# A fused perceiver layer on one core: another order of the first groups, of the passage between the stages and of the first loads

## What is computed

```python
# 1 cross attention of the normalised x (hc) with the context (hq)
Sim = (hc @ w1)[:, :, None] + (hq @ w2)[:, None, :] + einsum('bid,bjd->bij', hc * w3, hq) + b_sim[0]
hq_hat = softmax(Sim, axis=2) @ hq
hc_bar = softmax(max(Sim, axis=2), axis=1) @ hc
x = x + concat([hc, hq_hat, hc * hq_hat, hc * hc_bar]) @ W_qv + b_qv
# 2 gated linear recurrence over the 32 tokens, then a layer norm
xg = ln(x) * sigmoid(ln(x) @ Wg.T + bg)
s = s @ A + xg[t] * Bp;  y[t] = s @ Cp + Dp * xg[t]
x = x + ln(y + xg) * gamma + beta
# 3 feed-forward with ternary weights and a low-rank term
h = bitlinear(ln(x), w_fc) + gate * (ln(x) @ v.T @ fast_b.T @ u.T)
x = x + bitlinear(relu(h) ** 2, w_proj)
```

## Time and profile before

| | before |
|---|---|
| median of three runs | 493.66 us (492.95 to 495.50) |
| profiled execution: time / span | 493.86 us / 492.0 us |
| mean granted clock of TensorE | 0.995 |
| PE busy | 463.0 us (94%) |
| PE weight loads busy | 400.3 us (81%) |
| DVE / ACT / POOL busy | 397.6 / 362.6 / 340.6 us |
| moved by DMA | 70.40 MB, mean 143 GB/s |

### The profile page before, as it was taken

The page is one execution under the profiler, slowest core; times in us unless marked ns, Lnnn a source line. Parts: engine busy times, 40 slices in busy tenths (PEclk is TensorE's granted clock), DMA queues, the critical chain, the costliest instruction groups (busy, mean ns, idle before and its releaser), DMA issues. The chain is left out here.

```text
span 492.0 us, 13707 instructions
## 1 busy us (share of the span) xinstructions
PE 463.0 (94%) x4375; PEld 400.3 (81%) x4375; DVE 397.6 (81%) x1210; ACT 362.6 (74%) x882; POOL 340.6 (69%) x446
## 2 busy tenths in 40 slices
PE   4889999999999999999999999778999999999995
PEld 3578788888988989888898878666888888888884
DVE  2698888888989889889889875788768788797654
ACT  3768688787887878878788786646787786876752
POOL 2478897876767767677676776124889887887552
PEclk9999999999999999999999998999999999999999
DMA  6954575576847648566674756774011312301102
GB/s 218 312 183 137 164 233 163 193 217 167 239 142 204 187 138 237 150 193 183 169 215 129 194 130 163 141 250 148 0 47 40 88 40 48 87 10 35 44 1 85
DMA packets 77454, 70.40 MB, mean 143 GB/s; under 512 B 39476, under 2 KB 60232, under 8 KB 76872
## 3 DMA queue, kind: packets, MB, share of 16 engines
q1 hardware_dynamic: 77384, 69.54, 49.2%
HBM read 56.87 MB, written 12.65 MB: 141 GB/s over the span
## 5 line engine op out<-in xcount | busy, mean ns | idle before, releaser
L1871 POOL TENSOR_TENSOR sq_lo<-scan_x,sq_hi 128x512 fp32r<-128x512 f32 x63 | 82.9, 1318 | 32.8 <-ACT sq_hi L1826 32.8
L1026 ACT COPY ctxT<-turn_ps 128x512 f32<-128x512 f32 x128 | 68.9, 590 | 10.2 <-PE turn_ps L801 3.8
L1818 ACT ACTIVATE relu<-fc_ps,fc_square 128x512 f32<-128x512 f32 x64 | 43.8, 686 | 32.7 <-PE fc_ps L1740 32.6
L1916 DVE SCALAR_TENSOR_TENSOR scan_x<-fc_ps,relu 128x512 f32<-128x512 f32 x64 | 43.7, 685 | 26.0 <-ACT relu L1818 25.4
L1209 POOL TENSOR_TENSOR hb_lo<-hbT,hb_hi 128x256 fp32r<-128x256 f32 x32 | 24.2, 758 | 43.0 <-ACT hb_hi L1097 43.0
L1734 PE MATMUL fc_ps<-xn_hi,fc_T 128*128 128x512 f32 x128 | 51.6, 403 | 2.1 <-DVE scan_x L1916 2.1
L1195 POOL TENSOR_TENSOR rstd<-ve,neg_half 128x1 f32<-128x1 f32 x64 | 35.3, 552 | 23.1 <-DVE ve L1456 20.7
L801 PE MATMUL turn_ps<-ident,ctxn 128*128 128x128 f32 x352 | 49.1, 285 | 2.3 <-DMA ctxn<-in_ctx 1.7
L1734 PE MATMUL fc_ps<-xn_lo,fc_T 128*128 128x512 f32 x128 | 50.4, 394 | 0.0
L1201 POOL TENSOR_TENSOR proj_in<-proj_in,below 128x512 f32<-128x512 f32 x31 | 48.6, 1567 | 0.0
L801 PEld LDWEIGHTS turn_ps<-ident,ctxn 128*128 128x128 f32 x352 | 42.7, 151 | 2.9 <-DMA ctxn<-in_ctx 2.1
(11 more groups left out here) (253 smaller groups left out, 1448.0 us busy)
## 6 DMA issues: line engine op xcount, KB each, us to landing
ctxn<-in_ctx SPq DMA_DIRECT2D x22, 1024.0 KB, 5.5
toeplitz<-in_ctx SPq DMA_DIRECT2D x10, 1024.0 KB, 5.6
resid<-in_x SPq DMA_DIRECT2D x32, 128.0 KB, 5.5
ctx_end<-in_ctx SPq DMA_DIRECT2D x32, 128.0 KB
gated_tokens<-gated SPq DMA_DIRECT2D x32, 128.0 KB, 6.0
scan_x<-gated_tokens SPq DMA_DIRECT2D x60, 64.0 KB, 4.8
out<-resid SPq DMA_DIRECT2D x7, 512.0 KB, 3.3
scan_quarters<-scan_x SPq DMA_DIRECT2D x3, 1024.0 KB, 5.4
```

What stands on the lines that cost most here:

```text
L1026: act.copy(ctxT[:, b, :, 0:J - 1], turn_ps[b % 2][:, :].rearrange("p (k j) -> p k j", k=KD)).then_inc(ctxT_copied, 1)
L1818: act.activation(relu[m % 2], fc_ps[m % 2][:, :], ACT.Relu, scale=fc_square[:, m:m + 1]).then_inc(relu_done, 1)
L1871: pool.tensor_tensor(sq_lo[:, tile(c, m) % PARTS, :], sq[m % SQ], sq_hi[:, tile(c, m) % PARTS, :].bitcast(F32), ALU.subtract).then_inc(sq_ ...
L1916: dve.scalar_tensor_tensor(out=sq[m % SQ], in0=fc_ps[m % 2][:, :], scalar=0.0, in1=relu[m % 2], op0=ALU.max, op1=ALU.mult).then_inc(sq_don ...
```

## The change

- **First loads.** The first context comes in four DMAs, one per batch, each with a semaphore of its own. `w1` and `b_sim`, before loaded with one descriptor per partition, come as one row each and are spread by two products with `ones`. ctx(2) and x(3) are issued ahead of Wg, bg and b_qv.
- **Step 0 on PE** starts with ten transposes of the identity whose result nobody reads (`WARM_1`), and has four more (`WARM_2`) behind each part of the context. ACT copies the first part before it handles hc.
- **Steps 1 and 2.** The split of W_qv is mixed with the other work of step 1; `weigh_hc(1)` moves to DVE, `weigh_hc(2)` behind two copies; the turning and splitting of Wg and its first product of states move to step 2. POOL puts the 257th column first in every step.
- **Step 32 and the last group's gate.** `project_hc` goes ahead of the turn of z, `make_z(30)` behind `hb_hi`; the sum over `w_proj` goes ahead of `zT_lo`, and `scales` behind `gate_in`; `tanh_gate(31)` goes one block earlier.
- **Second block.** The first four y loads have two semaphores. The scan uses `proj_ps[0]` and `fc_ps` for n=8 to 11, `proj_ps[1]` for n=12 to 15; n=15 is done after the first two tiles of chunk 0. Eight unread transposes (`WARM`) precede `turn_first`. The squares live in `fc_in`, no longer in `scan_x`. `load_y(2)` no longer waits for the last scan copy. In chunk 0 DVE has another order. On the very last tile ACT rounds tile 6 before the relu of tile 7.

```diff
@@ sync: first loads
-                load_ctx(0)
-                sp.dma_start(ends[:, :], ctx[:, J - 1, :]).then_inc(consts_loaded, 16)
+                sp.dma_start(w1_row, row(w_sim[0:D])).then_inc(w1_loaded, 16)
+                sp.dma_start(bsim_row, row(b_sim)).then_inc(w1_loaded, 16)
+                for b in range(NB):
+                    if b == 2:
+                        sp.dma_start(ends[:, :], ctx[:, J - 1, :]).then_inc(consts_loaded, 16)
+                    sp.dma_start(ctxn[0][:, b, :, :], ctx[b, 0:J - 1, :].rearrange("(q t) d -> q t d", t=JT)
+                                 ).then_inc(ctx_first[b] if b < 3 else ctx_loaded[0], 16)
                 load_x(1)
-                sp.dma_start(w1_all[:, :], everywhere(w_sim[0:D])).then_inc(w1_loaded, 16)
-                sp.dma_start(bsim_all[:, :], everywhere(b_sim)).then_inc(w1_loaded, 16)
...
@@ tensor: step 0
                     if g == 0:
+                        for i in range(WARM_1):
+                            pe.transpose(qv_ps[:, 0:P], ident[:, :], ident[:, :])
                         pe.wait_ge(rows_loaded, 16)
-                        pe.transpose(gate_ps[:, 0:2 * KD], w_rows, ident[0:2 * KD, 0:2 * KD]).then_inc(rows_turned, 1)
-                        turn_hc(0)
-                    if has_a:
+                        pe.transpose(gate_ps[:, 0:2 * KD], w_rows, ident[0:2 * KD, 0:2 * KD])
+                        pe.wait_ge(w1_loaded, 16 * 2)
...
+                        pe.matmul(w1_ps, ones[0:1, :], w1_row, start=True, stop=True).then_inc(w1_placed, 1)
+                        for b in range(NB):
+                            pe.wait_ge(ctx_first[b] if b < 3 else ctx_loaded[0], 16)
+                            turn_context(0, b)
+                            if b == 0:
+                                turn_hc(0)
+                            if b == 2:
+                                turn_ends()
+                            for i in range(WARM_2):
+                                pe.transpose(qv_ps[:, 0:P], ident[:, :], ident[:, :])
...
@@ tensor: step 32
+                    if g == GROUPS:
+                        project_hc(g)
+                    elif has_c:
...
+                        if g < GROUPS:
+                            project_hc(g)
                         at_least(pe, hb_hi_ready, g)
                         project((hb_hi, hb_lo), 3, hb_lo_ready, g)
+                        if g == GROUPS:
+                            turn_z(g - 2)
...
@@ gpsimd: every step
+                    if has_a:
+                        place_end(g)
                     if has_b:
                         low_part(hc_lo[:, :, :], hc_probT[o][:, 0, :, :], hc_hi[:, :, :], hc_hi_ready, hc_lo_ready, g)
...
@@ vector: second block
...
             for h in range(2):
+                dve.wait_ge((y_first_half, y_loaded[0])[h], 16 * CH // 2)
...
@@ tensor: second block
+            third_banks, fourth_banks = (*proj_ps[0], *fc_ps), proj_ps[1]
+            FOURTH = (PIECES - 1) * BLOCKS
+            WARM = 8
...
+                    for i in range(WARM):
+                        pe.transpose(xt_ps[1][:, 0:P], ident[:, :], ident[:, :])
                     for h in range(2):
                         pe.wait_ge(xn_done, h + 1)
-                        if h == 0:
-                            pe.wait_ge(scan_copied, PIECES * BLOCKS)
...
-                for n in range(2 * BLOCKS, PIECES * BLOCKS):
+                for n in range(2 * BLOCKS, PIECES * BLOCKS - 1):
                     last_scan(n)
                 turn_first()
...
                             for i in range(2):
                                 hidden_low(0, i)
+                            last_scan(PIECES * BLOCKS - 1)
@@ scalar: second block
+                        if c == CHUNKS - 1 and m == MT - 1:
+                            square_hi(c, m - 1)
                         if has(c):
                             relu_tile(c, m)
```

315 lines of the change are left out of this document (184 added, 131 removed).

## The result

The changed kernel takes 490.97 us (median of 20 runs, 489.87 to 492.45) against 493.28 us before (20 runs): ratio 0.9948, 95% interval 0.9935 to 0.9962, so it is 0.52% faster. I had forecast 489.2 us, a gain of 4.5 us; the medians lie 2.3 us apart.

The account below looks back on a forecast made before the run. PE was taken to bound the kernel, busy 253.41 of 255.50 us in the steady groups. Start 2.6, passage 1.5 and tail 0.4 summed to 4.5 us, giving a median of 489.2 us; range 486.2 to 492.5.

Parts of the forecast that it names:

- the give-back in chunk 0: Second block, chunk 0: DVE's extra square and y moments, less two sums, make `ve_x` and `turn_in` later, -0.9 us.
- the steady groups: The 30 groups at PE's own pace: POOL's new order costs 0.2 us on an idle enough engine, so nothing changes.
- start, to group 3: Start: 2.25 + 0.65 + 1.5, less 1.8 that step 2 pays back, 2.6 us shorter; bounds -1.5 and 4.2.
- tail: Last tiles: `square_hi` of tile 6 no longer waits behind the relu, 0.4 us won (0 to 0.8).
- First score: Start: the score of group 0 ends at 11.75 instead of 14.00, gain 2.25 us, with PE's clock rising at 6.7.
- Context of group 1 "before 11.8": Start: without the two short-row loads the DMA hole closes and ctx(1) lands before 11.8 us, when PE asks.
- Groups 1 and 2: Steps 1 and 2: 0.65 us from `weigh_hc(1)` on DVE, 1.5 from overlapped rounding and subtraction, -1.8 paid back in step 2.
- The rival "steady groups get longer": POOL's new head delays `hc_lo`: 7 us over 29 groups from 0.24 each, 500.8 us at 0.4; chance 0.05.
- Step 32 and the gate: Step 32: filling the wait for z wins 1.3 us; a gate ready before the last scan products wins 0.55 more.
- Second block up to the low-rank product: Passage into the second block: with fewer waits for y loads and scan copies, `turn_first` comes 2.4 us earlier in all.
- The rival "the passage gives everything back in chunk 0": Chunk 0: the wait for `ve_x` pulls `norm_x` and the relus behind it, 490.7 us; chance 0.14.
- The clock, rule and row: Start: unread transposes count as busy time for PE's clock, against the skill's rule, with the rise at 6.7 us.

Follow-up runs that it names:

- the eight profiles with this list: Profiled executions of the whole change and follow-up kernels sharing its PE list up to the first score; that score ended between 12.35 and 13.71 us.
- one_load: The change with the first context loaded by one DMA again, the order of PE, ACT and DVE as in the change: 493.45 us, ratio 1.0003.
- rows_spread: The change with two loads of one short row per partition (w1, b_sim) back ahead of group 1's context: 493.01 us, ratio 0.9943.
- real_warm: The change with its unread transposes of step 0 replaced by unread float32 products: 490.74 us.
- pool_order_back: The change with POOL placing the 257th context column where it did before, from group 3 on: 490.93 us, ratio 0.9953.
- the three groups: Three occasions of four follow-up kernels each, with own runs of the kernel before: medians 493.1, 492.87 and 495.66 us.

## Why the prediction was right or wrong

The forecast was "faster", 4.5 us; it came out at 2.3 to 2.6 us (difference of the medians, ratio), inside the range of 486.2 to 492.5, and about half of the 4.5. The mechanisms of the gain are there; the terms that failed are the give-back in chunk 0 and the steady groups. In terms of the sum:

| term | forecast | measured |
|---|---|---|
| start, to group 3 | 2.6 | 3.5 |
| steady groups | 0 | -1.3 |
| step 32 to the low-rank product of chunk 0 | 2.4 | 2.9 |
| chunk 0 | -0.9 | -2.9 where the clock stays in the first interval, -4.4 in the profile |
| tail | 0.4 | 0.3 |
| sum | 4.5 | 2.5, by the -2.9 |

That the time still fell well inside the range is in part luck: the start and the passage came out 1.4 us better than forecast and paid for some of the 3.3 us that the other two terms missed.

- **First score, 2.25 forecast, 1.42 measured.** The clock rose at 8.7 where I had 6.7, and the score ended at 12.58 in place of 11.75. None of the eight profiles with this list had the rise at 6.7; their scores give gains of 0.3 to 1.65. (The upper bound of the start was added up wrongly: a score that ends at 10.95 gives 3.05 in place of 2.25, so 3.4 in all and not 4.2.) That the parts of the load matter was right (`one_load`).
- **Context of group 1 "before 11.8": wrong.** The hole closed as forecast, but the turn waited until 13.69 (in the nine other kernels with both edits it began between 12.05 and 13.91), so that the earlier weighing and copies of that group won less. `rows_spread` has it at 15.28, 1.6 us behind the whole change and 2.3 behind `real_warm`, and the slow clock behind that wait on top.
- **Groups 1 and 2.** The turn of group 2 came 4.42 us earlier, where my three terms make 4.4 (the list at the end of the prediction said 23.4; by its own sum it should have said 24.2). Step 2 gave back 0.90, not 1.8; which of its parts hid beside others I did not take apart. The start is 3.5 us shorter, forecast 2.6.
- **Steady groups, "nothing": wrong by 1.3 us.** My argument looked at POOL alone. The wait of POOL that moved was indeed long over in ordinary steps, which all stayed at 8.68 us; the loss is in six uneven steps, above all step 30. The rival "steady groups get longer" had the right place, but at 7 us and more over five times the loss, and its mechanism (the new head of POOL's step) is the one that `pool_order_back` rules out. What makes the steps longer is open.
- **Step 32 and the gate, 1.3 + 0.55: right.** From the turn of group 31 to the first scan products 17.36 became 16.31 (1.05), to the weights another 0.58; the one gap left is 1.01 us, forecast 0.9. To the start of the second block 1.90, forecast 1.85.
- **Second block up to the low-rank product.** Forecast 2.4 for the passage at the first turn; measured 3.3 there (322.76 against 328.31, less the 2.21 of the start) and 2.9 at the low-rank product (5.12 less 2.21). Right in kind, 0.5 low.
- **Chunk 0, -0.9: the step that failed.** Measured -4.4 in the profiled execution, -2.9 where the clock stays in the first interval. I had counted one square and the moments of y against two sums. Missing were the idle wait for the first relu (1.14), the additions that now run beside POOL (1.2 more for the four), and what a late `ve_x` does to PE: a gap of 2.52 us, behind which the clock falls (0.8 to 1.0). In the profiled execution the clock had also fallen ahead of it, behind the gap of 1.49 us (1.5 more). The runs put 1.6 to 2.2 us on DVE's order. The rival "the passage gives everything back in chunk 0" named the place and the engine; its 490.7 us is close to the 490.97 measured, but by luck: the start was 0.9 us better and the steady groups 1.3 us worse than either had them.
- **Tail, 0.4: 0.3.**
- **The clock, rule and row.** Unread transposes did not keep PE at half pace: in all eight profiles the rise falls between 8.4 and 11.0 us, in a stretch of transposes that runs from 5.54 on. The Trainium skill's rule ("TensorE: Matmul & The Clock Gate", Part 4: PE-mode transpose) that they do not count is not borne out here: with real products in place of the unread ones the rise was no earlier (between 9.97 and 11.70). But my own reading, that more of them bring the clock earlier, bought nothing either: without the 26 the first score was as fast and ended sooner.
- **Same clock or other clock.** Of the 20 runs of the change 3 had a mean clock under 0.993; of those of the kernel before 13 of 29, 6 of 23 and 11 of 18 in the three groups. At 0.995 the kernel before takes 491.9 to 494.1 us (13 runs of the three groups, median 492.37) and the change 489.9 to 491.0 (7 runs, median 490.70), 1.7 us apart where the medians are 2.3 apart. So a part of the measured gain, perhaps a quarter, is that the clock falls less often, which no term of my sum had; it is a reading of the runs' lists from different occasions, not an experiment.
